# A two-layer attention and mixture-of-experts kernel: gates spread by DMA instead of TensorE, one turn of q in the second attention, extra VectorE work dealt out over slots, another opening

## What is computed

```python
x = x + _L0_attn_a_ref(_layernorm(x), ...)   # 16 heads of 8, q and k RMS-normed
x = x + _L0_ffn_ref(_layernorm(x), ...)      # 8 experts, top 2, and a shared one
x = x + _L0_attn_b_ref(_layernorm(x), ...)   # differential attention, 16 maps, rotary
x = x + _L0_ffn_ref(_layernorm(x), ...)      # the same experts again

# the mixture, per token
scores = softmax(xt @ gate_w.T)              # top 2 of 8 kept as gates
xe = gate_e * xt
out = sum_e silu(xe @ w1[e]) * (xe @ w3[e]) @ w2[e]  +  the shared expert on xt

# the second attention
probs = softmax(q k^T)                       # 16 maps in 8 pairs
diff = probs[:, 0] - lam * probs[:, 1]
attn = rmsnorm(diff @ v) * (1 - LAMBDA_INIT)
```

## Time and profile before

| | us |
|---|---|
| median of 3 runs (lowest, highest) | 990.48 (988.3, 992.23) |
| the profiled execution | 989.17 |
| its span, first to last instruction | 987.4 |
| busy in the span: TensorE, VectorE | 874.8, 732.5 |
| busy in the span: ScalarE, GpSimd | 578.9, 528.6 |
| mean granted TensorE clock | 0.973 |

### The profile page before, as it was taken

One profiled execution on the slowest core, in us unless ns is written; L12 is line 12 of the kernel. 1 busy time (PEld: TensorE's weight loads), 2 busy tenths in 40 slices (PEclk: granted clock), 3 DMA queues, 4 the chain that ended last, 5 costly groups with the idle time before them and its releaser, 6 DMA issues.

```text
span 987.4 us, 22246 instructions
## 1 busy us (share of the span) xinstructions
PE 874.8 (89%) x7264; PEld 621.0 (63%) x7264; DVE 732.5 (74%) x1978; ACT 578.9 (59%) x903; POOL 528.6 (54%) x610
## 2 busy tenths in 40 slices
PE   2799999888999999999788888888878799999998
PEld 0355555545688777788555555555545688888887
DVE  4677777766777777777678898989883577767775
ACT  1478778766444434444488888888875344444443
POOL 4666666663444455554436575757542644454551
PEclk9999999988999999999899999999997899999999
DMA  8000000000000000000000000000000000000000
GB/s 235 1 2 1 0 0 0 0 2 2 1 1 1 1 1 0 0 1 1 1 2 1 1 0 0 0 0 0 1 1 1 1 12 12 12 7 4 11 11 23
DMA packets 14607, 8.70 MB, mean 9 GB/s; under 512 B 1616, under 2 KB 14160, under 8 KB 14544
## 3 DMA queue, kind: packets, MB, share of 16 engines
q1 hardware_dynamic: 12960, 7.28, 2.6%
q10 hardware_dynamic: 1584, 0.62, 0.2%
HBM read 5.80 MB, written 2.10 MB: 8 GB/s over the span
## 4 chain that ended last, share of the span: by engine, by line
PE 21%; issue 13%; DVE 11%; POOL 7%; ACT 2%; DVEq 0%; POOLq 0%; ACTq 0%
DVE s_qs L1088 6%; PE psum L819 5%; PE psum L787 5%; POOL f_xe_lo L1434 3%; POOL f_p L1444 3%; PE psum L1327 2%; PE psum L769 2%; PE psum L1289 1%; DVE f_xe L1471 1%; PE psum L885 1%; PE psum L1291 1%; PE psum L1290 1%; PE psum L874 1%; PE psum L804 1%; ACT f_xe_hi L1403 1%
## 5 line engine op out<-in xcount | busy, mean ns | idle before, releaser
L1403 ACT ACTIVATE f_xe_hi<-f_xe 128x512 fp32r<-128x512 f32 x128 | 80.9, 632 | 204.6 <-DVE f_xe L1471 204.6
L1434 POOL TENSOR_TENSOR f_xe_lo<-f_xe,f_xe_hi 128x512 fp32r<-128x512 f32 x64 | 83.9, 1311 | 184.6 <-ACT f_xe_hi L1403 184.6
L1088 DVE TENSOR_REDUCE s_qs<-psum 128x4 fp32r<-128x1024 f32 x128 | 156.3, 1222 | 35.4 <-PE psum L804 34.6
L1327 PEld LDWEIGHTS psum<-w,f_h 128*128 128x128 f32 x1152 | 147.7, 191 | 8.8
L1327 PE MATMUL psum<-w,f_h 128*128 128x128 f32 x1152 | 153.0, 276 | 0.0
L467 ACT ACTIVATE s_probs<-psum 128x1024 f32<-128x1024 f32 x128 | 125.9, 1023 | 33.1 <-PE psum L354 32.7
L955 ACT ACTIVATE s_probs<-psum 128x1024 f32<-128x1024 f32 x128 | 131.3, 1026 | 19.5 <-PE psum L787 17.8
L1289 PE MATMUL psum<-f_xe_hi,w_hi 128*128 128x512 f32 x288 | 127.0, 441 | 7.6 <-POOL f_xe_lo L1434 7.0
L1487 DVE TENSOR_TENSOR f_h<-psum,f_g 128x512 f32<-128x512 f32 x144 | 99.2, 689 | 44.9 <-ACT f_g L1388 34.6
L1291 PE MATMUL psum<-f_xe_lo,w_hi 128*128 128x512 f32 x288 | 114.1, 396 | 0.0
L1290 PE MATMUL psum<-f_xe_hi,w_lo 128*128 128x512 f32 x288 | 113.5, 394 | 0.0
(11 more groups left out here) (177 smaller groups left out, 1732.6 us busy)
## 6 DMA issues: line engine op xcount, KB each, us to landing
out<-x SPq DMA_DIRECT2D x8, 256.0 KB, 2.3
x<-in_x SPq DMA_DIRECT2D x3, 512.0 KB, 9.6
w<-in_w SPq DMA_DIRECT2D x3, 512.0 KB, 7.5
x<-in_x SPq DMA_DIRECT2D x2, 256.0 KB, 3.9
select_raw<-in_select SPq DMA_DIRECT2D x1, 512.0 KB, 4.8
rope_cos<-in_rope_cos SPq DMA_DIRECT2D x1, 256.0 KB, 3.9
rope_sin<-in_rope_sin SPq DMA_DIRECT2D x1, 256.0 KB, 4.6
wqkv_a<-in_Wqkv_aT ACTq DMA_DIRECT2D x1, 192.0 KB, 3.6
```

The costliest lines, as they stand in the source:

```text
L1088: dve.tensor_reduce(o[:, r:r + 2, 2 * p:2 * p + 2, 24:25].bitcast(F32R), room(km, i).rearrange("p (r j s) -> p r j s", r=2, j=2), AX.X, AL ...
L1327: ins = pe.matmul(Y[k % 2][:, t * P:(t + 1) * P], g.f_h[:, q, t * P:(t + 1) * P], g.w2[:, e, :], start=(e == 0 and t == 0), stop=(e == NE ...
L1434: pool.tensor_tensor(xe_lo[:, ring(e), :], src, xe_hi[:, ring(e), :], ALU.subtract).then_inc(xe_lo_pool.sem, 1)
```

## The change

**The opening** loads x in eight parts of four tiles, from the third on only when ScalarE's first loads have landed; statistics and roots come part by part at other heads, the last before k = 0 and at k = 0. ScalarE runs a tiny exponential before its small loads. VectorE, not GpSimd, does Newton's twelve steps for the first two sequences.

**First attention:** the weights' high parts are rounded at head 11 of k = 12 and 13, their low parts at head 5 of k = 13 and 14; `select` is gone; `wo` is scaled once.

**Second attention:** q is turned once, straight into `qt`; the maxima (L1088) go to a small tile `s_mxs`, TensorE turns 16 columns of it per half, ScalarE copies 16 rows of 128, and SP writes them by DMA into rows 24, 56, 88 and 120 of `qt`. The additions of epsilon for both roots move from VectorE to GpSimd.

**The mixtures:** VectorE turns the gates in blocks of 32 into `f_sg`; SP writes them to DRAM and broadcasts each expert's row of 512 gates to all partitions, into a ring of four SBUF tiles `gt`, which `scale` reads instead of SB. `spread`, `s_turn` and the copy `f_st` are gone. Normalisation, turn, logits, `best` and the power of a chunk happen one chunk earlier, `sums` and `gates` in slots 2 and 3 of the chunk before. Residual and statistics stand in slots 5 and 6, masks in slot 8. VectorE keeps the low parts of experts 2 and 3; GpSimd has seven, in the order 0, 1, 4, 5, shared, 6, 7, with the shared expert's input in slot 2. The power is one group of four in slot 7. The stores of the second mixture stand between the broadcasts.

```diff
-PARTS = ((0, 4), (4, 8), (8, 16), (16, 24), (24, 32))
-STATISTICS = ((-3, 0), (-2, 11), (-1, 12), (0, 8), (0, 12))
-ROOTS = ((-3, 0), (-2, 15), (-1, 15), (0, 15), (1, 5))
+PARTS = tuple((t, t + 4) for t in range(0, NT, 4))
+LOADED = ((0, 1), (1, 1), (2, 2), (2, 2), (3, 4), (3, 4), (3, 4), (3, 4))
+STATISTICS = {(-3, 0): (0,), (-3, 11): (1, 2), (-2, 3): (3,), (-2, 12): (4, 5), (-1, 12): (6, 7)}
+ROOTS = {(-3, 0): (0,), (-2, 5): (1, 2, 3), (-1, 5): (4, 5), (0, 5): (6, 7)}
...
         for i, (lo, hi) in enumerate(PARTS):
-            sp.dma_start(g.x[:, lo:hi, :], x_view[:, lo:hi, :]).then_inc(x_loaded[i], 16)
+            if i == 2:
+                sp.wait_ge(first_loaded, first_count)
+            sp.dma_start(g.x[:, lo:hi, :], x_view[:, lo:hi, :]).then_inc(x_loaded[LOADED[i][0]], 16)
...
+                act.wait_ge(filled, 1)
+                act.activation(tiny[:, 60:61], g.minus_half[:, 0:1], ACT.Exp)
...
+                if k in (13, 14) and h == 5:
+                    pool.wait_ge(w_hi_sb.sem, k - 12)
+                    w, hi, lo = ((g.w1, g.w1_hi, g.w1_lo), (g.w3, g.w3_hi, g.w3_lo))[k - 13]
+                    pool.tensor_tensor(lo[:], w[:], hi[:], ALU.subtract)
...
+                if km < NEWTON_ON_DVE:
+                    dve.wait_ge(seed.sem, seed.upto(m))
+                    i = 0
+                    for o, u, w, op in newton_steps():
+                        if i:
+                            dve.wait_ge(newton.sem, newton.upto(m, i))
+                        dve.tensor_tensor(o[:], u[:], w[:], op).then_inc(newton.sem, 1)
+                        i += 1
...
-            if k == 12:
-                dve.wait_ge(g.late_loaded, g.late_count)
-                dve.tensor_copy(g.w1_hi[:], g.w1[:]).then_inc(w_hi_sb.sem, 1)
-                dve.tensor_copy(g.w3_hi[:], g.w3[:]).then_inc(w_hi_sb.sem, 1)
-                dve.tensor_copy(g.select[:], g.select_raw[:])
             for h in part:
+                if k in (12, 13) and h == 11:
+                    dve.wait_ge(g.late_loaded, g.late_count)
+                    if k == 12:
+                        dve.tensor_scalar(g.wo[:], g.wo[:], 4 * (1.0 - LAMBDA_INIT), None, ALU.mult)
+                    w, hi = ((g.w1, g.w1_hi), (g.w3, g.w3_hi))[k - 12]
+                    dve.tensor_copy(hi[:], w[:]).then_inc(w_hi_sb.sem, 1)
...
-                    pe.wait_ge(qf_sb.sem, qf_sb.upto(n, i // 4 + 1))
+                    pe.wait_ge(row_sb[i // 4].sem, row_sb[i // 4].upto(n))
...
-                    ins = pe.matmul(room(km, i)[:, o:o + SEQ], qp[r:r + 24, q, c * P:(c + 1) * P],
+                    ins = pe.matmul(room(km, i)[:, o:o + SEQ], qt[r:r + 24, km % 2, q, c * P:(c + 1) * P],
...
-                turn(qs[:, km % 2], p).then_inc(qf_mm.sem, 1)
+                    pe.wait_ge(mt_sb.sem, mt_sb.upto(m, 1))
+                pe.transpose(QK[0:16, 0:P], mxs[:, km % 2, p].rearrange("p r j c -> p (r j c)"),
+                             g.identity[:]).then_inc(mt_mm.sem, 1)
...
-                        act.wait_ge(qf_mm.sem, qf_mm.upto(m, p + 1))
-                        act.activation(half(qt[:, km % 2], p), QK, ACT.Copy).then_inc(qf_sb.sem, 1)
+                        act.wait_ge(mt_mm.sem, mt_mm.upto(m, p + 1))
+                        act.wait_ge(row_sb[p].sem, row_sb[p].upto(m - 1))
+                        act.activation(mt[0:16, p, :], QK[0:16, 0:P], ACT.Copy).then_inc(mt_sb.sem, 1)
...
+                    pool.wait_ge(ms_sb.sem, ms_sb.upto(m))
+                    pool.tensor_tensor(g.s_var2[:], g.s_ms2[:], g.rms_eps[:], ALU.add).then_inc(var_sb.sem, 1)
...
+                    pool.wait_ge(mv_sb.sem, mv_sb.upto(m))
+                    pool.tensor_tensor(g.s_vare[:], g.s_mv[:, 0:2, 1], g.ln_eps[:], ALU.add).then_inc(vare_sb.sem, 1)
...
-                dve.tensor_reduce(o[:, r:r + 2, 2 * p:2 * p + 2, 24:25].bitcast(F32R),
+                dve.tensor_reduce(mxs[:, km % 2, p, r:r + 2, :, c:c + 1].bitcast(F32R),
...
-                dve.wait_ge(ms_sb.sem, ms_sb.upto(m))
-                dve.wait_ge(inv2_sb.sem, inv2_sb.upto(m - 1))
-                f = (1.0 - LAMBDA_INIT) ** -2
-                dve.tensor_scalar(g.s_var2[:], g.s_ms2[:], f / 16, f * RMS_EPS_B,
-                                  ALU.mult, ALU.add).then_inc(var_sb.sem, 1)
...
-                dve.tensor_scalar(g.s_vare[:], g.s_mv[:, 0:2, 1], LN_EPS, None, ALU.add).then_inc(vare_sb.sem, 1)
...
+    def sync(sp):
+        for m in range(NSEQ):
+            n = Step(None, 0, m)
+            for p in range(2):
+                sp.wait_ge(mt_sb.sem, mt_sb.upto(n, p + 1))
+                sp.dma_start(qt[24:P:32, m % 2, 2 * p:2 * p + 2, :].rearrange("r j (c t) -> r (j c) t", c=2).bitcast(F32),
+                             mt[0:16, p, :].bitcast(F32)).then_inc(row_sb[p].sem, 16)
...
-LOW_ON_DVE = (2, 5, 6, 7)
+LOW_ON_DVE = (2, 3)
+LOW_ON_POOL = (0, 1, 4, 5, 8, 6, 7)
...
-LEAD = {1: (0,), 3: (1,), 4: (2,), 6: (3,), 8: (4,), 9: (5,), 13: (6,), 15: (7,)}
+LEAD = {0: (0,), 2: (1,), 3: (2,), 5: (3,), 6: (4,), 7: (5,), 13: (6,), 15: (7,)}
...
-    "norm": 8, "x_turn": 0, "xt_sb": 0, "logits": 1, "best": 1, "pow": (2, 2, 2, 2), "gates": 5, "s_turn": 6,
-    "st_sb": 6, "residual": 0, "rstd": 0,
+    "norm": 4, "x_turn": 5, "xt_sb": 5, "logits": 6, "best": 7, "masks": 8, "pow": 7, "sums": 2, "gates": 3,
+    "residual": 5, "stats": 6, "rstd": 8, "shared": 2,
 }
-FF_LEAD = {"x_turn": 0, "xt_sb": 1, "logits": 2, "best": 2, "exp": 4, "gates": 5, "s_turn": 6, "st_sb": 6}
+FF_LEAD = {"x_turn": 0, "xt_sb": 1, "logits": 2, "best": 2, "masks": 2, "exp": 4, "sums": 5, "gates": 5}
...
+    def turned(n, k, e, task):
+        return ([(n + 1, k + 1)] if k == -1 and e == FF_LEAD[task] else []) + (
+            [(n + 2, k + 2)] if k + 2 < NCH and e == FF[task] else [])
...
+        return [x for x in ahead(n, k, e, 3) if x[2] < E] + ([(n, k, E)] if e == FF["shared"] and 0 <= k < NCH else [])
...
-            def spread(m, km, e):
-                if e == 0:
-                    if km == 0:
-                        pe.wait_ge(before.turned.sem, before.turned.upto(last))
-                    pe.wait_ge(st_sb.sem, st_sb.upto(m))
-                    pe.wait_ge(xe_sb.sem, xe_sb.upto(m - 1))
-                else:
-                    pe.wait_ge(xe_sb.sem, xe_sb.upto(m, e))
-                pe.matmul(SB, g.select[:, e, :], st[:, km % 2, :],
-                          start=True, stop=True).then_inc(sb_mm.sem, 1)
...
-            def s_turn():
-                pe.wait_ge(lo_sb.sem, lo_sb.upto(n + 1))
-                for t in range(4):
-                    ins = pe.transpose(T[:, t * P:(t + 1) * P], ssp[:, t, :], g.identity[:])
-                ins.then_inc(st_mm.sem, 1)
...
-                dve.tensor_tensor(xe[:, e % 2, :], SB, xt[:, km % 2, :], ALU.mult).then_inc(xe_sb.sem, 1)
+                dve.tensor_tensor(xe[:, e % 2, :], gt[:, e % 4, :], xt[:, km % 2, :], ALU.mult).then_inc(xe_sb.sem, 1)
...
+                dve.transpose(g.f_sg[:], g.f_m[:, 0, :, :].rearrange("p t e -> p (t e)")).then_inc(sg_sb.sem, 1)
...
+        def store(m):
+            view = out.rearrange("(n s) (c p) d -> n p (s c) d", s=2, p=P)
+            sp.wait_ge(x_sb.sem, x_sb.upto(Step(None, 0, m)))
+            sp.dma_start(view[m], g.x[:, 4 * m:4 * m + 4, :]).then_inc(stored, 16)
+        for m in range(NCH):
+            n = Step(None, 0, m)
+            sp.wait_ge(sg_sb.sem, sg_sb.upto(n))
+            sp.dma_start(g.gates[m % 2].rearrange("e (t b j) -> b (e t) j", t=4, b=4),
+                         g.f_sg[:]).then_inc(written.sem, 16)
+            sp.wait_ge(written.sem, written.upto(n))
+            for e in range(E):
+                if e >= 4 or m > 0:
+                    sp.wait_ge(xe_sb.sem, xe_sb.upto(n, e - 3) if e >= 4 else xe_sb.upto(n - 1, e + 5))
+                sp.dma_start(gt[:, e % 4, :], g.gates[m % 2, e].partition_broadcast(P)).then_inc(gt_sb[e % 4].sem, 16)
+                if not first and e == 3 and m >= 2:
+                    store(m - 2)
+        if not first:
+            for m in (NCH - 2, NCH - 1):
+                store(m)
+            sp.wait_ge(stored, 16 * NCH)
```

252 lines of the change are left out of this document (117 added, 135 removed).

## The result

The change made the kernel slower: 1064.64 us in the median of 4 runs (1062.02 to 1066.23), and the kernel before 990.99 in 4 runs; the ratio is 1.077, 95% interval 1.074 to 1.080. I had said 941 us, and faster with a chance of 0.94. The profiled execution has a span of 1060.2 us where that of before has 987.4.

What follows compares the result with a forecast made beforehand. Rings across engines, not TensorE alone, were taken as the bound. Mixtures -32, second attention -2, end of first attention -6, opening -8.5 and transitions -1 summed to -49.5 us, giving 941 us; own range 926 to 956, overall 907 to 967.

Steps and rivals of the forecast that it cites:

- (6): Mixtures, per chunk: scales reading two SBUF tiles contend with GpSimd's low parts; +0.4 us, plus +0.6 us for scale 6.
- (7): Mixtures, gates' path: DRAM write and broadcast take 5 us, hidden with 2 us to spare; GpSimd's added work hidden too.
- part (1): Mixtures, per chunk: spreads and gates' turn leave TensorE, the 4.05 us slot becomes a bare 2.6; -1.45 us.
- the rival that eats the gain: Mixtures: scales wait a whole low part three times a chunk, which saves 0.5 rather than 2.1 us; 965 us, chance 0.15.
- part (5): Mixtures, first one, per chunk: the shared expert's high part moves into a slot with a scale; +0.5 us.
- parts (2) and (3): Mixtures, per chunk: statistics apart from residual, -0.7 us (second mixture -0.35); `best` loses masks and its low part, -0.8 us.
- Late gates, as a rival: Mixtures: write and broadcast exceed 7.3 us and chunks stand; 1039 us at the upper bound, chance 0.04.
- TensorE's pace: Mixtures: VectorE's waits fall into its gaps, chunks fall to TensorE's busy time, 23.3 and 22.9 us; 916 us, chance 0.19.
- a ring through the power: Second attention: the ring through GpSimd's 2.91 us power holds, so a sequence changes by only -0.15 us, -2 us in all.
- The term of Newton's steps: Opening: twelve steps take 4.9 us on GpSimd, about half on VectorE; -2.5 us for two sequences.
- The lumps of statistics: Opening: two lumps at k = 0 go, one of them ahead of TensorE's 1.93 us wait; -3.5 us.
- the smaller powers: Opening: smaller powers stand ahead of the low parts; -1 us.

Runs made afterwards that it cites:

- the mended kernel: Changed kernel with one edit: GpSimd's low part waits for the count reached in the order ScalarE issues the high parts; 999.0 us, ratio to before 1.009.
- the shared part last: Changed kernel with the shared expert's high part issued behind expert 7's and its low part last on GpSimd, wait unchanged; 985.75 us, ratio 0.997.
- all three edits of the tables: Changed kernel with the shared expert's high and low parts last, normalisation in slot 2 and the statistics' power in slot 6; 968.4 us.
- the run with the lump: Weights' casts and low-part subtractions back at their old places, against the 964.4 us kernel with x held back, old statistics places, Newton on GpSimd; 970.9 us.
- The two versions that came of it: Changed kernel with low parts reordered, normalisation and statistics' power moved, Newton's steps and statistics as before; x not held back 963.1 us, held back 964.4 us.
- With late gates: Gates' last steps and transpose in slot 5 instead of 3, against the 968.4 us kernel with shared expert last, normalisation and statistics' power moved; 1030.8 us.

## Why the prediction was wrong, point by point

**The step that failed: GpSimd's queue in parts (6) and (7).** In (6) I wrote that scale 6 "meets two low parts back to back (5 and the shared one)", and in (7) I called what is added to GpSimd hidden, since it is busy for 16.5 of 25 us. Busy time was right (16.5 us in the window above). But the shared low part did not follow low part 5; it waited 4.66 us, and low parts 6 and 7 with it. I had followed the data (its high part is issued in slot 2, so it is ready) and not the number in the wait. That was to be read in the code: the wait of `low` with e + 1, the event of nine, and the new order. The term was 0, and is 65 us; without it the changed kernel is at 999 us.

That leaves 58 us to the forecast's 941. By the stretches of the mended kernel's trace (70.7, 201.6, 258.7, 271.4 and 195.0 us) against those of before with their forecasts, the first mixture is over by 22.6, the second by 18.6, the opening by 12.8, the end of the first attention by 2.8 and the second attention by 1.7. The points that follow are about these.

**The crowded slot, part (1).** I let the long slot of the earlier trace rows become "a bare one of 2.6" and never listed what VectorE's table puts there now. The gates' last steps in slot 3 and the normalisation ahead of `f_h` in slot 4 fall into the same gap of 1.2 us: 4.70 us in the mended kernel, 3.91 with the shared part last, and the normalisation alone was worth some 13 us by ratios (985.75 to 971.0 on two chips).

**The port, part (6).** For scale 6 I took 0.6, with bounds of 0 and 1.3; measured are 1.51 - 0.68 = 0.83 for the scale and 0.79 for its slot. The size was right. Of scales 1, 2, 5 and 7, for which I had 0.4, only scale 5 is stretched in that chunk (1.25 us); the other three take 0.68. That the normalisation beside a low part doubles as well, 1.1 to 2.06 us, was missed. The mean of a scale is 718 ns in the changed kernel and 814 with the count mended: the stall had kept the two engines apart. With the shared part last it is 720 although the stall is gone too, so it is the low part put in between that meets the scales. As the rival that eats the gain it was worth 0.8 us of a slot where it was tried. Its 965 us did not follow from its own numbers either: three waits of 1.27 are 3.8 us, 2.8 more than the sum had, which is 42 us over the 15 chunks of the sum and not 24.

**The shared expert's high part, part (5):** right. Booked at 0.5 us, it is worth 0.43 in the slot that it leaves and 0.51 in the slot that it enters when it is moved.

**The stats slot and `best`, parts (2) and (3).** In the mended kernel they last 3.33 and 3.25 us; forecast were 2.95 and 3.2. The first has an `f_vare` of 0.81 us beside a low part, and the gap that I gave `stats`, 1.3 us, is 1.19 by its own rows (418.18 - 416.99). Together with a slot of the sums of 3.56 us instead of some 3.0 (scale 5 beside a late low part 4, which the powers of 6.9 us and the one behind them push back), the crowded slot and some tenths in others, they make up the 27.9 of that chunk against the forecast's 24.9. With all three edits of the tables the first mixture's chunk is at 25.5 and the second's at 25.2, within 0.6 us of the forecast's 24.9 and 24.65: most of that gain was to be had, but the tables of the change did not have it.

**The gates' DMAs, part (7):** right for the steady chunks. 5.2 to 5.4 us against 5, and no wait in them. The one of 4.3 us at the start of the second mixture was in no term; what it costs was not tested. Late gates, as a rival, stood at 1039 us, near the time that was measured; the mechanism had no part in it.

**TensorE's pace (rival, 916 us):** not met. Its busy time fell to 23.8 us as worked out, and chunks stayed at 25.2 us and above.

**The second attention:** the forecast of -2 us was met in the trace (271.7 to 269.7), but that says little: in the other eleven kernels with the same program for this stage the stretch is between 265.6 and 272.3 us. And its reasons do not hold. I held that a ring through the power paces it and that the mean's copy inherits the wait of `s_vare`. Without the power the stage is only 5.9 us shorter, and the copy takes 0.2 to 0.3 us:

```profile
L1186 DVE COPY mean<-s_mv x16: 169/217/321, 579.2 to 835.6; 128x2 f32 x10, 128x2 f32<-128x2 f32 x6
```

**The end of the first attention:** forecast -6; -5.1 in the trace, 6.4 by the run with the lump. Right, in place and size.

**The opening:** forecast -8.5, measured +4.1. The first turn did come forward by the 1.5 us, from 9.15 to 7.66. It was the held-back x that did it, not the table: with the early table load alone it stood at 9.25, and only the projection behind it came 0.2 us sooner (10.51 for 10.67). The term of Newton's steps failed: GpSimd's 4.9 us ran beside VectorE's next normalisation, and on VectorE 3.1 us stand ahead of it. I had seen that ("VectorE's next x is then later") and booked -2.5 for two sequences all the same; the run with the steps back on GpSimd puts them at +5 to +7. The lumps of statistics, at -3.5, gave nothing that any run shows, and the smaller powers, at -1, were not tried apart.

**The range** (907 to 967) took in the unknown prices and no mistake in the code. No rival was a wait by number, and that was the one that decided.

## What to carry to other kernels

A wait on a counting semaphore names a place in the releasing engine's program order, not a piece of data. When a change reorders what increments it, every wait on it has changed, in lines that the diff does not show: write down the new order and recompute each count, those that are merely too high above all, since they are safe and silent. Then lay out the new slots one by one with all that the tables put between two dependent steps, because the gain of a removed wait is only as large as the next fullest slot lets it be. The two versions that came of it, with the low parts' order restored, three numbers of a table moved and Newton's steps and the statistics back in their places, are 2.4 and 2.5% faster than the kernel before where the change as it stood was 7.7% slower.

## What the runs showed of the hardware

A stall of 4.6 us before TensorE was followed by some six us at the lower clock (matmuls of 0.63 us instead of 0.39), and with the stall the lower clock went: 0.90 to 1.00 in the window of a chunk. With late gates it came again: 3.58 us of standing, then matmuls of 0.63 us, and 0.90 in the chunk. A stall in the middle of a chunk thus looks like two troubles and is one. A write of 16 KB to DRAM and a broadcast of 256 KB from it take 5.4 us from issue to use, 1.93 of them for the write. Four normalisations of 128x128, 1.11 us alone, take 2.06 beside one GpSimd subtraction of 1.33. On GpSimd a power of 128x16 takes 2.91 us and a product of the same two tiles 0.22. And an engine's late start can hide contention: with GpSimd's queue mended, scales were on average 0.1 us longer (814 ns for 718), since the two engines now met; with the shared expert's low part in another place they were not (720).
